# A graph network layer on one core: the rounds of the edge attention written out in full, gathers that read their indices in place, and the transposed one-hot made by ScalarE in four parts

## The reference

```python
q, k, v = ((xn @ W.T + b).reshape(bs, 8, 32) for W, b in (q, k, v))
qe, ke, ve = q[dst], k[src], v[src]            # one row per edge
sim = einsum('hed,hed->eh', qe, ke) * scale
p = exp(sim - segment_max(sim, dst)[dst])
agg = segment_sum(p * ve, dst) / segment_sum(p, dst)
x = x + agg @ Wo.T + bo + linear_attention(xn)
x = x + experts(layernorm(x))
```

## Time and profile before

| | |
|---|---|
| median of three runs | 1167.2 us |
| the profiled execution, its own time | 1167.8 us, span 1166.1 us |
| the attention stage | about 208 to 846 us of the span |
| VectorE busy | 871.2 us, 75% of the span |
| TensorE busy | 906.9 us, 78% |
| GpSimd busy | 682.6 us, 59% |
| ScalarE busy | 484.8 us, 42% |
| the gathers (L986) | 408, some 1.05 us each on GpSimd |
| the index copies (L971) | 408, 81.5 us busy |
| the comparison (L1075) | 28, 21.4 us busy |

### The profile page before, as it was taken

The page is one execution under the profiler, slowest core; times in us unless marked ns, Lnnn a source line. Parts: engine busy times, 40 slices in busy tenths (PEclk is TensorE's granted clock), DMA queues, the critical chain, the costliest instruction groups (busy, mean ns, idle before and its releaser), DMA issues. The chain is left out here.

```text
span 1166.1 us, 17876 instructions
## 1 busy us (share of the span) xinstructions
PE 906.9 (78%) x4059; PEld 627.4 (54%) x4060; DVE 871.2 (75%) x1761; ACT 484.8 (42%) x1312; POOL 682.6 (59%) x1043
## 2 busy tenths in 40 slices
PE   4889876487787677777777778777766499999995
PEld 3445453365555555555555555555544366666664
DVE  3888867699999899889988999999758434433333
ACT  3566535355454345434543554454422123333330
POOL 2533375778888888878887888886000403233311
PEclk9999968788989799879987989899878699999998
DMA  4344264467777676767766666665042333333300
GB/s 149 102 100 99 81 196 120 133 179 206 201 196 208 184 204 189 190 170 187 188 176 167 185 172 184 173 173 152 11 137 86 104 107 117 111 132 117 121 29 8
DMA packets 79901, 167.53 MB, mean 144 GB/s; under 512 B 15515, under 2 KB 47006, under 8 KB 79550
## 3 DMA queue, kind: packets, MB, share of 16 engines
q0 software_dynamic: 38464, 110.26, 35.4%
q1 hardware_dynamic: 39431, 54.81, 14.9%
q10 hardware_dynamic: 1904, 1.45, 0.4%
HBM read 163.32 MB, written 18.95 MB: 156 GB/s over the span
## 5 line engine op out<-in xcount | busy, mean ns | idle before, releaser
L986 POOL DMA_INDIRECT slot<-kv_d,idx x320 | 335.6, 1049 | 59.6 <-issue 40.0
L1230 PE MATMUL at_pa<-at_pv,at_hot 128*125 128x264 f32 x880 | 271.3, 452 | 98.2 <-DVE agg L1111 97.2
L1230 PEld LDWEIGHTS at_pa<-at_pv,at_hot 128*125 128x125 f32 x880 | 176.8, 216 | 170.8 <-DVE agg L1111 108.6
L1016 ACT ACTIVATE at_hot<-iota_w,nloc_e 128x125 f32<-128x125 f32 x440 | 139.4, 387 | 141.1 <-PE at_pa L1230 137.6
L1220 PE MATMUL at_pq<-q,at_hotT 125*128 x1320 | 179.4, 295 | 15.9 <-issue 10.2
L1220 PEld LDWEIGHTS at_pq<-q,at_hotT 125*128 125x128 bf16 x1320 | 133.6, 105 | 47.9 <-issue 21.0
L1088 DVE TENSOR_REDUCE at_sc<-at_prod 128x32 f32<-128x1024 f32 x110 | 133.6, 1214 | 2.0
L1639 POOL DMA_INDIRECT out<-slot,node_s x32 | 32.0, 1001 | 166.4 <-DVE slot L1671 124.5
L1097 DVE TENSOR_TENSOR at_pv<-slot,at_pp 128x1056 f32<-128x1056 f32 x88 | 109.4, 1243 | 18.2 <-issue 16.9
L1660 DVE TENSOR_TENSOR y<-xp,b 128x256 f32<-128x256 f32 (+1 forms) x32 | 13.6, 425 | 139.1 <-PE xp L1706 139.1
L1081 DVE TENSOR_TENSOR at_prod<-at_pq,slot 128x1024 f32<-128x1024 f32 x88 | 107.3, 1219 | 9.1 <-PE at_pq L1220 8.3
(11 more groups left out here) (322 smaller groups left out, 1406.7 us busy)
## 6 DMA issues: line engine op xcount, KB each, us to landing
slot<-in_w SPq DMA_DIRECT2D x16, 1024.0 KB, 7.5
locrow<-loc_d SPq DMA_DIRECT2D x28, 500.0 KB
slot<-kv_d,idx POOLq DMA_INDIRECT x320, 3.8
kv_d<-vst SPq DMA_DIRECT2D x25, 128.9 KB
base<-in_x SPq DMA_DIRECT2D x5, 625.0 KB
kv_d<-kst SPq DMA_DIRECT2D x25, 125.0 KB
row_d<-base SPq DMA_DIRECT2D x5, 625.0 KB
out<-base SPq DMA_DIRECT2D x1, 3125.0 KB
```

The lines of the kernel that those rows point to most:

```text
L986: pool.indirect_dma_start(m.quads[r][:, i, :], None, m.kv_d, bass.IndirectOffsetOnAxis(ap=m.idx[:, r, i:i + 1].bitcast(U32), axis=0), boun ...
L1016: last = act.activation(hot[:, u % 8, :], m.iota_w[:, :], ACT.Abs, bias=at(m.nloc_e, c)[:, u:u + 1])
L1230: mm = pe.matmul(pa[p % 2][:, 0:H * VW], hot[:, u % 8, :], pv[:, u % 8, :, :].rearrange("p h c -> p (h c)"), start=(u % 2 == 0), stop=(u % ...
```

## The change

`rounds` and the loops go: each engine's 30 bodies are written out, so that every chunk number is a constant. The gather reads its index column out of `src_e` in place; the tile `idx` and the copies go. `hotT` is made by ScalarE, quad by quad, in four parts: an Abs of (partition number - local number) in place in `locrow`, a wait on the new semaphore `loc_far`, and Relu(1 - that) into `hotT`. `hotT_made` now counts quads; TensorE waits for its own quad only, a part waits until TensorE has spread the same quad of the chunk before, and SP loads the next row after the fourth part. The parts of chunk n + 1 stand in ScalarE's `body(n)` behind the Exp, behind `hots(c, 1)`, behind `borders(n)` (and `cleared`) and behind `hots(c, 2)`. In VectorE's body `product(n, 3)` takes the place of the comparison. The diff, without the hunks that only drop the loop's arguments:

```diff
@@ -53,11 +53,10 @@
 EPS = 1e-5
 AT_CONST = 5
 SOON = 8
-RING, LOOP, TURN = 10, 3, 5
-LOOPS = (CH - LOOP - 5) // TURN
+RING = 10
 SPILL = 32
 EARLY = U * KV - NT * (2 * HID + 1)
-assert EROWS * W2 >= E and EROWS % 2 == 0 and PAIRS % 2 == 0 and REST == U // 2 and (CH - LOOP - 5) % TURN == 0 and QUADS * TURN % RING == 0 and CAP == 489
+assert EROWS * W2 >= E and EROWS % 2 == 0 and PAIRS % 2 == 0 and REST == U // 2 and RING > 2 * QUADS and CAP == 489
 
 
 def spread(ap, axis, n):
@@ -917,23 +916,13 @@
 
             return not isinstance(c, int) or (0 <= c < CH and q < quads(c))
 
-        def rounds(eng, body):
-
-            for n in range(LOOP):
-                body(n, n, 0)
-            with eng.Fori(0, LOOPS) as k:
-                for s in range(LOOP, LOOP + TURN):
-                    body(TURN * k + s, s, k)
-            for n in range(CH - 5, CH + 2):
-                body(n, n, 0)
-
-        def place(s, q):
-
-            return (QUADS * s + q) % RING
-
-        def use(s, q, k):
-
-            return QUADS * TURN // RING * k + (QUADS * s + q) // RING
+        def place(n, q):
+
+            return (QUADS * n + q) % RING
+
+        def use(n, q):
+
+            return (QUADS * n + q) // RING
 
         def windows_of(chunk, pairs, engines):
 
@@ -947,11 +936,12 @@
                 sp.dma_start(m.first_rows.rearrange("p (t d) -> p t d", t=SOON), m.base[:, 0:SOON, :]).then_inc(S.spilled, 16)
                 sp.dma_start(m.wo_d.rearrange("p (c n) -> p c n", c=2), m.woT[:, :, :]).then_inc(S.spilled, 16)
 
-                def body(n, s, k):
+                def body(n):
                     if exists(n) and not (isinstance(n, int) and n == 0):
-                        wait(sp, S.hotT_made, n)
+                        wait(sp, S.hotT_made, QUADS * n)
                         sp.dma_start(locrow[:, :], loc_c[bass.ds(n, 1), :].to_broadcast([TT, U * 128])).then_inc(S.loc_in, 16)
-                rounds(sp, body)
+                for n in range(CH + 2):
+                    body(n)
                 sp.wait_ge(S.pv_made, QUADS * (CH - 1) + quads(CH - 1))
                 sp.dma_start(m.woT[:, :, :], m.wo_d.rearrange("p (c n) -> p c n", c=2)).then_inc(S.reloaded, 16)
                 sp.dma_start(m.base[:, 0:SOON, :], m.first_rows.rearrange("p (t d) -> p t d", t=SOON)).then_inc(S.reloaded, 16)
@@ -966,39 +956,21 @@
                 pool.iota(sign[:, 1:2], pattern=[[0, 1]], base=0, channel_multiplier=1, allow_small_or_imprecise_dtypes=True).then_inc(S.at_const, 1)
                 add_mixed(pool, m, SOON, NT)
 
-                def index(c, s, u):
-                    r = place(s, u // 4)
-                    pool.tensor_copy(m.idx[:, r, u % 4:u % 4 + 1], at(m.src_e, c)[:, u:u + 1]).then_inc(S.idx_ready, 1)
-
-                def gather(c, s, steps):
-                    for u in range(steps):
-                        q, i = u // 4, u % 4
-                        r = place(s, q)
-                        if i == 0:
-                            pool.wait_ge(S.idx_ready, U * c + u - 2 * U + 4)
-                            pool.nop(nofuse=True)
-
-                            if s == 2 and q < 2:
-                                pool.wait_ge(S.spilled, 32)
-                            else:
-                                pool.wait_ge(S.pv_made, QUADS * c + q + 1 - RING)
-                            pool.nop(nofuse=True)
+                def gather(c, q):
+                    r = place(c, q)
+                    if QUADS * c + q < RING:
+                        pool.wait_ge(S.spilled, 32)
+                    else:
+                        pool.wait_ge(S.pv_made, QUADS * c + q + 1 - RING)
+                    pool.nop(nofuse=True)
+                    for i in range(4):
+                        u = 4 * q + i
                         pool.indirect_dma_start(m.quads[r][:, i, :], None, m.kv_d,
-                                                bass.IndirectOffsetOnAxis(ap=m.idx[:, r, i:i + 1].bitcast(U32), axis=0),
+                                                bass.IndirectOffsetOnAxis(ap=m.src_e[:, c, u:u + 1].bitcast(U32), axis=0),
                                                 bounds_check=N - 1, oob_is_err=False).then_inc(S.arrived[r], 16)
-                        if u + 8 < steps:
-                            index(c, s, u + 8)
-                        elif steps == U:
-                            index(c + 1, s + 1, u + 8 - U)
-                for u in range(8):
-                    index(2, 2, u)
-                gather(2, 2, U)
-                with pool.Fori(0, LOOPS) as k:
-                    for s in range(LOOP, LOOP + TURN):
-                        gather(TURN * k + s, s, U)
-                for c in range(CH - 5, CH - 1):
-                    gather(c, c, U)
-                gather(CH - 1, CH - 1, U - REST)
+                for c in range(2, CH):
+                    for q in range(quads(c)):
+                        gather(c, q)
 
             @block.scalar
             def _(act):
@@ -1041,8 +1013,20 @@
                         act.activation(m.agg[:, g * LG:(g + 1) * LG].rearrange("p t h c -> p (t h c)"),
                                        m.one_col[0:TT, :].to_broadcast([TT, words]), ACT.Copy, scale=0.0).then_inc(S.agg_zero, 1)
 
-                def body(n, s, k):
+                def turned_hots(n, q):
+
+                    four = slice(4 * q * 128, 4 * (q + 1) * 128)
+                    if q == 0:
+                        act.wait_ge(S.loc_in, 16 * n + 16)
+                    act.activation(locrow[:, four], locrow[:, four], ACT.Abs, bias=m.iota_p[0:TT, 0:1], scale=-1.0).then_inc(S.loc_far, 1)
+                    act.wait_ge(S.loc_far, QUADS * n + q + 1)
+                    wait(act, S.q_spread, QUADS * (n - 1) + q + 1)
+                    act.activation(flat(hotT[:, 4 * q:4 * q + 4, :]), locrow[:, four], ACT.Relu, bias=m.one_col[0:TT, 0:1],
+                                   scale=-1.0).then_inc(S.hotT_made, 1)
+
+                def body(n):
                     c, b = n - 1, n - 2
+                    follows = exists(n) and exists(n + 1)
                     if exists(b, 3):
                         hots(b, 3)
                     if exists(c):
@@ -1056,30 +1040,36 @@
                         act.activation(fall2[0:1, :], fell[:, :], ACT.Exp, scale=-float(HD) ** -0.5).then_inc(S.chain_act, 1)
                         act.wait_ge(S.chain, CHAIN * c + SHIFT)
                         act.activation(bm[:, :], bm[:, :], ACT.Exp, scale=float(HD) ** -0.5).then_inc(S.chain_act, 1)
+                    if follows:
+                        turned_hots(n + 1, 0)
+                    if exists(c):
                         hots(c, 1)
+                    if follows:
+                        turned_hots(n + 1, 1)
                     if exists(n):
                         borders(n)
                     if isinstance(n, int) and n == 0:
                         cleared()
+                    if follows:
+                        turned_hots(n + 1, 2)
                     if exists(c, 2):
                         hots(c, 2)
+                    if follows:
+                        turned_hots(n + 1, 3)
+                for q in range(QUADS):
+                    turned_hots(0, q)
                 act.wait_ge(S.at_const, AT_CONST)
-                rounds(act, body)
+                for n in range(CH + 2):
+                    body(n)
 
             @block.vector
             def _(dve):
-                def turned_hots(n):
-
-                    dve.wait_ge(S.loc_in, 16 * n + 16)
-                    wait(dve, S.q_spread, QUADS * n)
-                    dve.tensor_scalar(flat(hotT[:, :, :]), locrow[:, :], m.iota_p[0:TT, 0:1], None, ALU.is_equal).then_inc(S.hotT_made, 1)
-
-                def product(n, s, k, q):
-                    dve.wait_ge(S.arrived[place(s, q)], 64 * use(s, q, k) + 64)
+                def product(n, q):
+                    dve.wait_ge(S.arrived[place(n, q)], 64 * use(n, q) + 64)
                     dve.wait_ge(S.q_spread, QUADS * n + q + 1)
                     wait(dve, S.reduced, QUADS * n + q)
                     dve.tensor_tensor(prod[:, :, :], pq[q % 2].rearrange("p (i d) -> p i d", i=4),
-                                      m.quads[place(s, q)][:, :, 0:D], ALU.mult).then_inc(S.prod_made, 1)
+                                      m.quads[place(n, q)][:, :, 0:D], ALU.mult).then_inc(S.prod_made, 1)
 
                 def reduce(n, q):
                     dve.wait_ge(S.prod_made, QUADS * n + q + 1)
@@ -1175,16 +1165,16 @@
                     if exists(c):
                         maxima(c)
                     if exists(n, 1):
-                        product(n, s, k, 1)
+                        product(n, 1)
                         reduce(n, 1)
 
                     if exists(c, 0):
-                        weigh(c, s - 1, 0)
+                        weigh(c, 0)
                     if exists(b, 3):
                         wins = windows(b, 3)
```

(36 more changed lines are left out.)

## The result

The changed kernel took 1148.5 us (median of 4 runs, 1146.2 to 1153.6), the kernel before 1164.8 in the same comparison (4 runs): a ratio of 0.9875, 95% interval 0.983 to 0.992. The forecast was 1141, range 1126 to 1162. The profiled execution took 1148.2 us (span 1146.5), against 1167.8 for the profiled one of before: 19.6 us less, where the sum said 25.9.

The account below looks back on a forecast made before the run. VectorE was taken as the bound in the attention stage, with GpSimd close behind. Rounds written out -22.9, comparison off VectorE -11 and start +8 gave -25.9 us, so 1141 us; 8-in-10 range 1126 to 1162.

Parts of the forecast that it names:

- the third rival: VectorE's 0.66 us a round is lost entirely, to gathers or to TensorE after the new order: 1152 us; 15%.
- Rounds written out: Attention stage: three loop-jump rounds of about 29 us become rounds of 21.68, -22.9 us (bounds -20.0 and -24.3).
- Gathers in place: GpSimd: 0.08 to 0.10 us less per gather, round 20.5 to 20.8 us; nothing itself, but lets the comparison's gain through.
- The comparison leaves VectorE: VectorE rounds: of 0.66 us each, 0.56 kept in 11 or 12 and 0.33 in 13 or 14, -11 us (0 to -18.5).
- ScalarE's parts: ScalarE: four Abs and Relu parts, 0.71 us an operation, 5.6 us a round, fit its idle time at no cost.
- Steady rounds: nothing: After the start, ScalarE's parts cost VectorE nothing; bound 0 to +0.2 us a round.
- The locrow ring: One-buffer row load plus ScalarE's parts: 19.3 us at an 8 us load, under VectorE's 21.25, so not binding.
- The start: ScalarE's parts of chunk 1 delay the first row copy to 237.1, and VectorE's carries: +8 us (+4 to +11).
- The second: Writing out saves nothing: the stall is instruction supply and the longer program pays it elsewhere, 1164 us; 10%.
- The first: The locrow ring or ScalarE becomes the bound and the kernel is slower, 1180 us; 8%.
- the fourth: Better: start costs half, VectorE keeps most of its 18.5 us, TensorE keeps its clock, 1130 us; 12%.

Follow-up runs that it names:

- e2: Kernel before with rounds written out and gathers reading src_e in place, the comparison staying on VectorE; 1136.6 us, ratio 0.9769.
- e1: Kernel before with only its rounds written out; comparison on VectorE and index copies stay; 1153.6 us, ratio 0.9942.
- e11: Changed kernel with GpSimd's index copies put back; 1158.9 us, ratio 0.9956.
- e9: e2 with VectorE's comparison covering only 16 of 2048 columns from chunk 1 on (result not the layer's); 1144.0 us, ratio 0.9828.
- e10: Changed kernel with an unused comparison of the same size back on VectorE and product(n, 3) behind the second add; 1151.3 us, ratio 0.9896.
- e3: Changed kernel with ScalarE's round 0 doing borders and cleared before the four parts of chunk 1; 1147.1 us, ratio 0.9861.
- e12: e2 with TensorE's turn of the row ends between the two pairs of sums of quad 2; 1128.4 us, ratio 0.9712.

## Why the prediction was right, and where not

The range and the sign held, but the 1141 us did not: the profiled pair gained 19.6 us and not 25.9, and the range held because it was wide enough to take in the third rival. One term, VectorE's 11 us, was nearly all wrong; 2.3 us gained behind the last scan, which no term names, and 1 us less at the start hid part of it. The terms:

- **Rounds written out, -22.9.** Right in the sum: no standstill is left on the first two chips, and e2's 25 rounds average 21.70, the 21.68 of the forecast (in the slowest of its five executions; by the ratio, e2 gained 27 us). But it needs the gathers in place. The prediction saw that GpSimd's 22.0 us are more than VectorE's 21.68 and that it "catches up during the three stalls", and then wrote "On the path it is worth nothing itself" of the gathers. Removing the stalls removes the catching up. Measured: 0.6% for the writing out alone (e1), 1.7% for the gathers on top (e2), 0.8% lost when they are taken back (e11).
- **Gathers in place.** The pitch is 1.30 us, as forecast (20.8 a round). (Before, the four parts of the earlier trace rows add up to 1.37 us; 1.38 is the distance of the starts, and sixteen are 22.1.) "Nothing on the path" was wrong, as just said.
- **The comparison leaves VectorE, -11.** This step failed. It took 0.56 us for clean rounds and 0.33 for long ones; measured are -0.38 for clean rounds, up to +0.5 for long ones and -1.7 us over 25 rounds (21.61 each against the 21.68 of before without its jumps), and no gain when the work is taken away or put back alone (e9, e10). Two things took it. In a clean round the forecast left about 0.1 us of waiting, before the product; the wait is 0.46 us, 0.35 more than before, and stands before the row. In the long rounds I had let the low clock give back part of the gain; in fact the shorter VectorE round goes with a lower clock (e9, and the changed kernel against e10).
- **ScalarE's parts, 0.** Their size was right, 0.71 and 0.72 us: ScalarE's two groups over the span, as the earlier trace rows.

```profile
L1024 ACT ACTIVATE at_hotT<-locrow,one_col 125x512 bf16<-125x512 bf16 x112 | 80.8, 722 | 3.6
...
L1021 ACT ACTIVATE locrow<-locrow,iota_p 125x512 bf16<-125x512 bf16 x112 | 79.3, 708 | 27.4 <-DMA locrow<-loc_d 23.8 <-PEq L687 3.6
```

  Of e2 to e10 a difference of 1.3% remains, of which the 7.9 us of the later start (scans at 232.5 and 240.4) are 0.7%. The rest can't be read off these two profiles (e2's was the slowest of its five runs). But e3, whose start is as early as e2's, is still 0.9% slower than e2 (0.9861 against 0.9769, intervals 0.9813 to 0.9909 and 0.9734 to 0.9805). So the late start is not most of the loss, and the forecast's "Steady rounds: nothing" is doubtful: something that came with the move costs there. Whether it is ScalarE's parts, the order on VectorE, TensorE's wait for each quad or the later load of the row was not separated.
- **The locrow ring.** It does not bind: outside the start, part 0 waits for its load 13 times, about 1 us each, in time that ScalarE has.
- **The start, +8.** Right: the row copy came at 236.0 (237.1 forecast), VectorE waited 4.9 us for it, and the second scan is 7.0 us later. Taking this away (e3) changed the time by 0.1% alone, within the intervals. ScalarE's timeline there:

```profile
227.34 6.05 ACT L1013 ACTIVATE agg<-one_col 125x1320 f32<-125x1320 f32 x5
...
236.03 0.36 ACT L1034 ACTIVATE at_row<-at_pchain 1x256 f32<-1x256 f32 x1
```

Of the rivals the third, VectorE's 0.66 lost entirely, 1152 us, describes what happened, with 15% against 55% for the forecast; it named gathers or the new order as the cause, and neither is needed: e9 loses it in the old order, and GpSimd waits for VectorE, not VectorE for gathers. The second (nothing saved by writing out, 1164) is refuted by e2 and, on the second chip, by e12, while the third chip does show slower written-out kernels, for a cause that stays open. The first and the fourth did not occur. The Trainium skill's rule (ScalarE: Activation LUTs, Rules for kernel authors) to keep Relu and its like on VectorE points the right way: e2, which does so, is 1.1% faster than the whole change. The reason it gives, the speed per element, is not what decided: VectorE's time was worth nothing that e9 and e10 could show.

## What to carry to other kernels

Before you count a gain on the busiest engine, look at the clock of the engine that it waits for and test with a dummy of the same size: if putting the work back costs nothing, moving it is useless and only its side effects remain. When a stall goes, ask who had used it to catch up. The one edit that removed a wait of VectorE for TensorE (e12: 0.6% over e2, within the intervals, and 2.0% on the third chip, clear of them) was worth more than the two that shortened VectorE's own work (the changed kernel against e10, and e9).

## What was not expected of the hardware

- With less work on VectorE the mean clock of TensorE was lower: 0.92 to 0.89 between 262 and 800 us (e2, e9), for the same matmuls and with TensorE's busy time up from 417.3 to 427.3 us.
- The kernel before took 1163 us on two chips and 1323 on a third, and there a change that gains 1.2% elsewhere loses 6.5%, with a standstill of VectorE of up to 9.4 us a round for which the profile shows no cause.
